# A quantised feed-forward stage: root mean square in the scale, more work on GpSimd, turned h one step later

## What is computed

```python
def rmsnorm(x, w):
    v = jnp.mean(jnp.square(x.astype(jnp.float32)), axis=-1, keepdims=True)
    x_hat = x * jax.lax.rsqrt(v + EPS_NORM)
    return (x_hat * w).astype(x.dtype)

def activation_quant(x):
    scale = 127.0 / jnp.clip(jnp.max(jnp.abs(x), axis=-1, keepdims=True), EPS_Q, None)
    return jnp.clip(jnp.round(x * scale), -128, 127) / scale
...
h = bitlinear(x, norm1_w, w1)
h = act_scale * jnp.square(jax.nn.relu(h)) + act_bias
y = bitlinear(h, norm2_w, w2)
```

## Time and profile before

| | us |
|---|---|
| median of 3 runs | 2208.47 |
| lowest, highest | 2199.37, 2210.56 |
| the profiled execution, its own time | 2208.38 |
| its span in the profile | 2206.4 |
| busy in the span: PE, DVE, ACT, POOL | 1934.4, 1438.6, 988.2, 937.7 |
| the last stage, first sum of squares to the end | 2018.5 to 2206.4 |

### The profile page before, as it was taken

How to read it: one execution, slowest core, us unless ns; L and a number is a source line. 1 busy time by engine, 2 the same in 40 slices (tenths; PEclk the granted TensorE clock), 3 DMA queues, 4 the chain that set the end, 5 groups by cost and what they waited for, 6 DMA issues and landing times. The chain is left out here.

```text
span 2206.4 us, 60606 instructions
## 1 busy us (share of the span) xinstructions
PE 1934.4 (88%) x21423; PEld 1458.4 (66%) x21426; DVE 1438.6 (65%) x3456; ACT 988.2 (45%) x1977; POOL 937.7 (42%) x978
## 2 busy tenths in 40 slices
PE   6999997997999489929999779999999999984675
PEld 3666666886888467728888657666767667652333
DVE  3666664775777634426676546776767777754998
ACT  2444442443111033413453335555555555534997
POOL 0111111221577723345655135656565565632333
PEclk8999997998999689968999879999999999985555
DMA  6211004995222199733331101101010101000111
GB/s 199 82 33 33 28 29 162 329 329 202 61 52 53 32 279 299 234 96 98 102 98 62 41 29 35 33 29 37 25 37 26 35 26 35 21 9 28 57 57 43
DMA packets 157099, 192.84 MB, mean 87 GB/s; under 512 B 27971, under 2 KB 140614, under 8 KB 157013
## 3 DMA queue, kind: packets, MB, share of 16 engines
q1 hardware_dynamic: 146741, 189.09, 27.3%
q0 software_dynamic: 10272, 2.62, 0.6%
HBM read 140.81 MB, written 77.51 MB: 99 GB/s over the span
## 5 line engine op out<-in xcount | busy, mean ns | idle before, releaser
L2960 DVE TENSOR_REDUCE xa_kq<-xa_A 100x4 f32<-100x1444 f32 x128 | 212.6, 1661 | 158.4 <-PE xa_A L2629 158.4
L2788 ACT ACTIVATE xa_prob<-xa_A 121x1600 f32<-121x1600 f32 x96 | 144.5, 1505 | 234.5 <-PE xa_A L2656 234.5
L2863 POOL TENSOR_TENSOR xa_prob<-xa_prob,xa_exp_bias 121x1600 f32<-121x1600 f32 x64 | 228.9, 3576 | 41.0 <-ACT xa_prob L2788 41.0
L1425 POOL DMA_INDIRECT slot_rows<-rt_x_again,rt_slot_u x150 | 155.2, 1035 | 67.7 <-issue 63.1
L2656 PEld LDWEIGHTS xa_A<-xa_q2T,xa_kqT 17*121 17x121 f32 x3072 | 92.3, 184 | 46.8 <-issue 29.7
L2888 POOL TENSOR_TENSOR xa_o_rstd<-xa_o_var,xa_power 100x1 f32<-100x1 f32 x32 | 17.8, 557 | 240.6 <-DVE xa_o_var L3000 240.6
L2629 PE MATMUL xa_A<-xa_kqT 16*100 16x361 f32 x1024 | 113.0, 511 | 6.8 <-ACT xa_prob L2788 6.8
L1671 POOL DMA_INDIRECT contrib<-ex_y,ex_place_u x64 | 62.4, 975 | 119.9 <-ACT ex_y L1723 107.1
L2656 PE MATMUL xa_A<-xa_q2T,xa_kqT 17*121 17x100 f32 x3072 | 108.5, 278 | 4.8 <-DVE xa_kq L2960 4.2
L717 DVE TENSOR_TENSOR sa_masked<-sa_A,sa_later_keys 100x1600 f32<-100x1600 f32 x32 | 58.4, 1824 | 73.1 <-PE sa_A L471 73.1
L2573 PE MATMUL xa_C<-xa_wk,xa_rows_T 128*121 128x256 f32 x384 | 103.7, 408 | 1.7 <-ACT xa_rows_T L2768 1.7
(11 more groups left out here) (353 smaller groups left out, 5115.9 us busy)
## 6 DMA issues: line engine op xcount, KB each, us to landing
ex_w<-in_w13T SPq DMA_DIRECT2D x64, 352.0 KB, 8.6
contrib<-xs_zero SPq DMA_DIRECT2D x30, 640.0 KB, 6.6
la_rows<-contrib SPq DMA_DIRECT2D x16, 1200.0 KB
xs_ctxT<-in_ctxT SPq DMA_DIRECT2D x32, 512.0 KB
xa_rows_t<-in_ctx SPq DMA_DIRECT2D x96, 121.0 KB
ex_w<-in_w2T SPq DMA_DIRECT2D x64, 176.0 KB
slot_rows<-xs_zero SPq DMA_DIRECT2D x32, 272.0 KB, 4.3
ex_x_t<-slot_rows SPq DMA_DIRECT2D x64, 136.0 KB, 6.1
```

What stands on the lines that cost most here:

```text
L1425: nc.gpsimd.indirect_dma_start(slot_rows, bass.IndirectOffsetOnAxis(slot_u[:, k, n:n + 1], 0), x_again[:, k, :], None, bounds_check=SLOTS ...
L2788: nc.scalar.activation(prob[:, n, :].rearrange("p (h a) -> p h a", h=HPG), A[:ROWS, :, 0:G * T], ACT.Exp, scale=EXP_SCALE).then_inc(exp_re ...
L2863: nc.gpsimd.tensor_tensor(chunk, chunk, exp_bias[:, n, :].unsqueeze(1).to_broadcast([ROWS, HEADS, T]), ALU.mult).then_inc(biased, 1)
L2960: nc.vector.tensor_reduce(kq[:T, k, NCH, 4 * j:4 * j + 4, DH:DH + 1].rearrange("p h o -> p (h o)"), A[:T, :, 0:src_len], axis=AXIS_X, op=A ...
```

## The change

The root mean square no longer multiplies x and h on VectorE. Rounding x/max(x) is the same with or without a common positive factor, so VectorE now scales the weighed but not normalised values, and the root enters the factors: `roots` raises the mean square to -0.5 and to 0.5 in one instruction of four numbers, `weigher` holds the first times the mean of the weights and the second times epsilon/127, and `scales` and `weigh` use them. `weigh_x` (x times weight) is on GpSimd, `weigh_h` stays on VectorE without the root. `whole_x` and `whole_h` go to GpSimd, `copy_x` goes from ScalarE to VectorE. `xn` and `hn` have two buffers each. TensorE and `copy_h` treat the h of the step before; `root_out` is one step later and first in GpSimd's list; `residual` comes behind `scale_h`. Line numbers after the change differ: `finish` is L3404, `weigh_h` L3376, `whole_h` L3202.

```diff
         ss = s.sb("ss", [P, 2, 2])
-        ms = s.sb("ms", [P, 2])
-        rms = s.sb("rms", [P, 2, 2])
-        power = s.sb("power", [P, 2])
+        ms = s.sb("ms", [P, 2, 2])
+        root = s.sb("root", [P, 2, 2])
+        factor = s.sb("factor", [P, 2, 2])
+        weigher = s.sb("weigher", [P, 2, 2, 2])
...
                 def rows(b):
                     k = b[1] % 2
                     sp.wait_ge(xn_ready, at(b, 1, -1))
+                    sp.wait_ge(x_squared, at(b, 1, -1))
                     sp.dma_start(x_t[:, k, :], x_tiles[b[0] * 2 + b[1]]).then_inc(x_loaded[k], 16)
...
             @block.gpsimd
             def _(pool):
-                for sem in (o_var_ready, o_rstd_ready):
+                for sem in (o_var_ready, o_rstd_ready, xn_ready, xi_ready, hi_ready):
                     pool.sem_inc(sem, LEAD)
                 pool.sem_inc(backw_ready, LEAD - 3)
-                nc.gpsimd.memset(power[:], -0.5)
+                nc.gpsimd.memset(power[:, 0, :], -0.5)
+                nc.gpsimd.memset(power[:, 1, :], 0.5)
+                nc.gpsimd.memset(factor[:, 0, :], 1.0)
+                nc.gpsimd.memset(factor[:, 1, :], EPS_Q / 127.0)
                 nc.gpsimd.memset(eps[:, 0:2], EPS_N)
                 nc.gpsimd.memset(eps[:, 2:3], LN_EPS).then_inc(power_set, 1)
                 pool.wait_ge(power_set, 1)
+                nc.gpsimd.tensor_tensor(factor[:, 0, :], factor[:, 0, :], wmean[:], ALU.mult).then_inc(power_set, 1)
+                pool.wait_ge(power_set, 2)
+
+                def weigh_x(b):
+                    k = b[1] % 2
+                    pool.wait_ge(x_loaded[k], loads_of(b, 1))
+                    nc.gpsimd.tensor_tensor(xn[:, k, :], x_t[:, k, :], n1[:], ALU.mult).then_inc(xn_ready, 1)
 
                 def weigh(b, has):
                     k = b[1] % 2
                         pool.wait_ge(relu_done, at(later(b, 1), 1, 1))
                     if has(-2):
                         pool.wait_ge(r_ready, at(later(b, -2), 1, 1))
-                    nc.gpsimd.tensor_tensor(backw[:, k, two], back[:, two], wmean[:, two], ALU.mult).then_inc(backw_ready, 1)
+                    pool.wait_ge(rms_ready, at(later(b, -1), 1, 1))
+                    if has(3):
+                        pool.wait_ge(x_turned, at(later(b, 2), 1, 1))
+                        pool.wait_ge(x_scaled, at(later(b, 3), 1, 1))
+                    nc.gpsimd.tensor_tensor(backw[:, k, two], back[:, two], weigher[:, 1 - k, 0, two], ALU.mult).then_inc(backw_ready, 1)
+
+                def whole_x(b):
+                    k = b[1] % 2
+                    nc.gpsimd.tensor_scalar(xi[:], xn[:, k, :], ROUND, 127.0, ALU.subtract, ALU.min).then_inc(xi_ready, 1)
+
+                def whole_h(b):
+                    k = b[1] % 2
+                    pool.wait_ge(h_turned, at(b, 1, 0))
+                    pool.wait_ge(h_scaled, at(b, 1, 1))
+                    nc.gpsimd.tensor_tensor(carry[:], eps[:, 0:1], eps[:, 0:1], ALU.add)
+                    nc.gpsimd.tensor_scalar(hi[:], hn[:, k, :], ROUND, 127.0, ALU.subtract, ALU.min).then_inc(hi_ready, 1)
 
                 def roots(b, has):
                     k = b[1] % 2
                     if has(1):
                         pool.wait_ge(h_summed, at(later(b, 1), 1, 1))
                     if b[1] > FIRST:
+                        pool.wait_ge(root_ready, at(later(b, -1), 1, 1))
+                    for copy in range(2):
+                        last = nc.gpsimd.tensor_tensor(ms[:, copy, two], ss[:, k, two], eps[:, two], ALU.add)
+                    last.then_inc(ms_ready, 1)
+                    pool.wait_ge(ms_ready, at(b, 1, 1))
+                    if b[1] > FIRST:
                         pool.wait_ge(rms_ready, at(later(b, -1), 1, 1))
-                    nc.gpsimd.tensor_tensor(ms[:, two], ss[:, k, two], eps[:, two], ALU.add).then_inc(ms_ready, 1)
-                    pool.wait_ge(ms_ready, at(b, 1, 1))
-                    if has(-1):
-                        pool.wait_ge(hn_ready, at(later(b, -1), 1, 1))
-                    if has(2):
-                        pool.wait_ge(xn_ready, at(later(b, 2), 1, 1))
-                    nc.gpsimd.tensor_tensor(rms[:, k, two], ms[:, two], power[:, two], ALU.pow).then_inc(rms_ready, 1)
+                    nc.gpsimd.tensor_tensor(root[:, :, two], ms[:, :, two], power[:, :, two], ALU.pow).then_inc(root_ready, 1)
+                    pool.wait_ge(root_ready, at(b, 1, 1))
+                    if has(-1) or has(2):
+                        pool.wait_ge(back_ready, at(later(b, -1), 1, 1))
+                    nc.gpsimd.tensor_tensor(weigher[:, k, :, two], root[:, :, two], factor[:, :, two], ALU.mult).then_inc(rms_ready, 1)
 
...
                 def body(b, has):
+                    if has(-2):
+                        root_out(later(b, -2))
+                    if has(4):
+                        weigh_x(later(b, 4))
                     if has(0) or has(3):
                         weigh(b, has)
+                    if has(3):
+                        whole_x(later(b, 3))
+                    if has(0):
+                        whole_h(b)
                     if has(1) or has(4):
                         roots(b, has)
-                    if has(-1):
-                        root_out(later(b, -1))
 
                 periods(pool, NT, FIRST, LAST, REACH, body)
 
                     last.then_inc(y_done, 1)
 
                 def body(b, has):
-                    if has(0):
-                        turn_h(b)
+                    if has(-1):
+                        turn_h(later(b, -1))
+                    if has(2):
+                        hidden(later(b, 2))
+                    if has(-1):
+                        down(later(b, -1))
                     if has(3):
                         turn_x(later(b, 3))
-                    if has(0):
-                        down(b)
-                    if has(3):
-                        hidden(later(b, 3))
 
                 periods(pe, NT, FIRST, LAST, REACH, body)
 
             @block.scalar
             def _(act):
-                for sem in (x_squared, relu_done, h_squared, h_summed, h_ready, xiT_ready, hiT_ready):
+                for sem in (x_squared, relu_done, h_squared, h_summed, h_ready, hiT_ready):
...
 
-                def copy_x(b):
-                    act.wait_ge(x_turned, at(b, 1, 1))
-                    act.wait_ge(h_done, at(b, 1, 0))
-                    nc.scalar.activation(xiT[:].rearrange("p c t -> p (c t)"), TX[:, 0:KC * P], ACT.Copy).then_inc(xiT_ready, 1)
-
                 def relu(b, slot):
...
                         relu(later(b, 1), k)
                     if has(1) or has(4):
                         if b[1] >= FIRST + 2:
-                            act.wait_ge(rms_ready, at(later(b, -2), 1, 1))
+                            act.wait_ge(ms_ready, at(later(b, -2), 1, 1))
                     if has(4):
                         square_x(later(b, 4), k)
+                    if has(-1):
+                        copy_h(later(b, -1))
                     if has(1):
                         square_h(later(b, 1))
                         sum_h(later(b, 1), k)
                         scale_h(later(b, 1))
-                    if has(0):
-                        copy_h(b)
-                    if has(3):
-                        copy_x(later(b, 3))
 
                 periods(act, NT, FIRST, LAST, REACH, body)
 
             @block.vector
...
-                def norm_h(b, slot):
+                def copy_x(b):
+                    dve.wait_ge(x_turned, at(b, 1, 1))
+                    dve.wait_ge(h_done, at(b, 1, 0))
+                    nc.vector.tensor_copy(xiT[:].rearrange("p c t -> p (c t)"), TX[:, 0:KC * P]).then_inc(xiT_ready, 1)
+
+                def weigh_h(b):
                     k = b[1] % 2
                     dve.wait_ge(h_ready, at(b, 1, 1))
-                    dve.wait_ge(rms_ready, at(later(b, -1), 1, 1))
-                    dve.wait_ge(hi_ready, at(b, 1, 0))
-                    nc.vector.scalar_tensor_tensor(hn[:], h[:, k, :], rms[:, slot, 0:1], n2[:], ALU.mult, ALU.mult).then_inc(hn_ready, 1)
-
-                def norm_x(b, slot):
-                    k = b[1] % 2
-                    dve.wait_ge(x_loaded[k], loads_of(b, 1))
-                    dve.wait_ge(rms_ready, at(later(b, -4), 1, 1))
-                    dve.wait_ge(xi_ready, at(b, 1, 0))
-                    nc.vector.scalar_tensor_tensor(xn[:], x_t[:, k, :], rms[:, slot, 1:2], n1[:], ALU.mult, ALU.mult).then_inc(xn_ready, 1)
+                    dve.wait_ge(hi_ready, at(later(b, -2), 1, 1))
+                    nc.vector.tensor_tensor(hn[:, k, :], h[:, k, :], n2[:], ALU.mult).then_inc(hn_ready, 1)
 
...
-
-                def scales(b, has):
+                    nc.vector.tensor_reduce(amax[:, 1:2], xn[:, k, :], axis=AXIS_X, op=ALU.max, apply_absolute_value=True).then_inc(x_max, 1)
+
+                def scales(b, has, slot):
                     two = pair(has, 0, 3)
```

(31 more changed lines are left out.)

24 lines of the change are left out of this document (14 added, 10 removed).

## The result

The change makes the kernel slower by 3.8%: 2290.1 us (2286.57 to 2294.01 in 4 runs) against 2209.5 of the kernel before on the same chip (2199.37 to 2212.87 in 4 runs), ratio 1.038 with an interval of 1.035 to 1.041. The forecast was 2218.4 with 2193 to 2243 as its range, so the time lies far above it, and also above the 2250 of rival 2.

A forecast was written before the change was run, and what follows sets the result against it. VectorE was taken to bound the kernel, ScalarE next; a new ring through GpSimd sums to 7.22 us a step against 6.77, so 0.45 x 22 = 10 us lost: 2208.4 + 10 = 2218.4 us, range 2193 to 2243.

The forecast's parts named there:

- rival 2: GpSimd's `tensor_scalar` costs what its two-input work costs: `whole_h` 2.31 us, 8.69 us a step, 2250 us; chance 0.20.
- What bounds the kernel before: Last stage: VectorE runs through, busy 47.21 of 50 us, ScalarE next at 45.57; steps 6.77 us apart.
- the ring of the new order: Last stage, once per step: `finish`, scales, GpSimd's passes, `ms`, root, `o_rstd`, `finish`; 7.22 us against 6.77.
- `whole_h` 1.05: GpSimd's pass taking the offset out of h, 1024 wide, in the ring: 1.05 us.
- `whole_x` 0.40: GpSimd's pass taking the offset out of x, 256 wide, in the ring: 0.40 us.
- the 7.22: Sum in us of the ring's seven links, one step of the last stage, against 6.77 before.
- `weigh_h` holds up `ms`, 1.10: VectorE's `weigh_h` takes the ports when `whole_h` ends, so GpSimd's `bf_ms` waits 1.10 us in the ring.
- exclude each other for their whole length: Port rule for VectorE and GpSimd instructions: the blocked one pays only its streaming part afterwards.
- ScalarE, TensorE and SP at nothing: Last stage: ScalarE's 5.79 us fits the longer step, TensorE's new order is hidden, SP's extra wait long satisfied.
- C: Theory in the follow-up runs: new order, copy of x or root of four numbers causes the loss; h_dve over 2265 us.
- Rival 1: The ports don't bind in the ring; ScalarE's 6.1 us sets the step, 15 us gained, 2193 us; chance 0.24.
- Rival 3: Shifting turned h only lengthens the tail, or next x waits for `copy_x`: 0 to +8 us; chance 0.04.

The follow-up runs named there:

- x_dve: Changed kernel with only the offset of x taken out by VectorE again, h's pass still on GpSimd: 2264.0 us, ratio to before 1.021 to 1.028.
- h_cast: Changed kernel with GpSimd's pass over h as a plain copy to bf16, offset and upper bound left out: 2240.3 us, ratio to before 1.009 to 1.016.
- h_sub: Changed kernel with GpSimd's pass over h as a subtract of a constant tile, upper bound left out: 2276.4 us, ratio to before 1.025 to 1.032.
- h_dve: Changed kernel with only the offset of h taken out by VectorE again: 2211.5 us, ratio to before 0.9994 to 1.0031.
- turn_back: hx_dve with the turning of h, its product and ScalarE's copy back in the step that scales h: 2211.7 us, ratio to before 0.9983 to 1.0018.
- hx_dve: Changed kernel with the offsets of both h and x taken out by VectorE again: 2202.9 us, ratio to before 0.9956 to 0.9980.
- f16_new: Changed kernel with scaled values written as fp16 plus 1536, offset taken off in the PSUM copies, no bound of 127: 2187.6 us, ratio to before 0.9855 to 0.9913.
- ints8: Changed kernel with VectorE scaling x and h into 8-bit integers and GpSimd only copying them to bf16: 2246.3 us, ratio to before 1.013 to 1.018.
- price: Kernel before plus extra GpSimd instructions on idle buffers, alone and beside VectorE, to tell durations: one run, 2248.2 us.
- b_h: Kernel before with one edit, the offset of h taken out by GpSimd behind the weighing of the scales: 2295.0 us, ratio to before 1.034 to 1.041.

## Why the prediction was wrong, point by point

- **What bounds the kernel before, and the ring of the new order**: right. Every link of the ring is in the trace in the place foretold; `finish` is held by `weigh_x` (0.70 to 0.81 us for 0.40), `backw` arrives behind `scale_h` and ends 0.05 us behind it, `o_rstd` to `o_rstd` closes once a step.
- **The step that failed** is the term `whole_h` 1.05 (and `whole_x` 0.40) with its bounds. It was put between "from below: the memsets" and "from above: the two-input instructions", 0.95 to 2.31 us, by the thought that an instruction with one tensor can't cost more than one with two. It took 3.62 (and 1.07): +2.57 and +0.67 of the 2.69 us by which the turn of 9.91 missed the 7.22, with 0.55 us in gaps, in `backw` and in the root, less the 1.10 of the collision that didn't come. The same two passes are what the forecast missed by pricing the first and last steps at nothing: behind the last `bf_hi` the span is 2.9 us longer, and the pass itself is 2.9 longer (3.62 for 0.69); ahead of the first it is 2.7, which is gone in x_dve (its stage begins 16.5 us ahead of the first `bf_hi`, the changed kernel's 20.1, that of before 16.7). The ends of a range that come from other operations don't bound this one, since here the operation sets the rate: two constants 3.63, one 2.78, none 1.04, for the same tile. The Trainium skill ("GPSIMD Engine Reference", section "Engine selection") calls one-input work roughly line-rate. The copy (1.04 us for 1024 elements) goes well with that; the arithmetic with constants is at 2.7 to 3.5 times its time. The measurement decides, and the estimate of 0.85 us from that page would have missed by more.
- **`weigh_h` holds up `ms`, 1.10**: right as a mechanism and in size (0.98 in h_cast and h_sub), absent in the changed kernel itself, where the pass outlasts the multiply.
- **"A VectorE `tensor_scalar` ... or one with two SBUF inputs, and a GpSimd instruction exclude each other for their whole length"**: too wide. It holds for GpSimd's two-tensor subtract, where VectorE ended 1.07 and 0.55 us behind 2.34, and there the Trainium skill ("SBUF — State Buffer", section "Who interferes with whom"), by which the first gets the pair for the whole instruction, agrees. Neither this nor that rule holds for its pass with constants, where the measurement decides: VectorE's instructions ended 1.5 to 2.5 us before GpSimd's.
- **ScalarE, TensorE and SP at nothing**: right for the loss (C fell with h_dve). The turning of h one step later isn't nothing where both passes are on VectorE: turn_back shows it there as a gain of 4 to 7 us. That the ring hides it in the changed kernel is argued, not shown.
- **The rivals**: rival 2 named the mechanism (GpSimd's `tensor_scalar` is dear) and stopped at the two-input rate, so its 8.69 us a step and 2250 fell short of 10.1 and 2290. It had 0.20; "against: those all read two tensors" was the wrong reason to keep it low. Rival 1 had one part right: `whole_h` does let VectorE's multiply through, after 1.0 us, and so the 1.10 is not in the ring. Its gain didn't follow, as the pass alone cost 2.57 more, and `finish` (0.83 for 0.78), h_cast's and h_sub's rows show that the ports do bind elsewhere. Rival 3 did not occur: in hx_dve, with the new order and both passes on VectorE, the first `bf_hi` comes 16.1 us into the stage and the last 10.1 before its end, for 16.7 and 10.1 in the kernel before.
- **The range** was built from the same two bounds, so it could not hold the time.

## What to carry to other kernels

An instruction that has no row of its own on that engine has no upper bound from its neighbours; before a large tile is moved to GpSimd, one kernel with the very form, alone and beside VectorE, prices it (here 3.63 us against VectorE's 0.69). An offload pays only if the other engine's queue has nothing behind it that the first engine waits for: VectorE was rid of 1.5 us of work a step (and got 0.3 of copying) and the step grew by 3.3, because the root that it waits for stood behind the pass. And look whether a pass can go altogether: letting the format of the write round, and the copy that exists anyway take the offset off, was faster in f16_new than every placement of the pass that was tried.

## What the runs showed of the hardware that was not expected

- GpSimd, 128 partitions by 1024 elements from fp32, alone: subtract and minimum with two constants 3.63 to 3.65 us, subtract with one 2.78, subtract of two tiles 2.34, copy to bf16 1.04; a copy from 8-bit integers took 1.03 in ints8. By the two widths of the first, (3.63 - 1.07) / 768 = 3.3 ns an element. Output in fp32 or bf16 made no difference. Once it had started, VectorE beside it lengthened it little or not at all (3.63 in price and the changed kernel, 3.63 to 3.70 in b_h); the 256-wide one took 1.52 in h_dve, where VectorE's `bf_hi` was in its way.
- While that pass runs, VectorE's instructions that share ports with GpSimd are held only until about 1.0 us after its start (price, x_dve). That this is close to the 1.04 us of the bare copy may mean that its reading is over by then; no run here tests it.
- VectorE's write to fp16 of a value near 1536, and to 8-bit integers, rounds to whole numbers at no extra time (0.748 us for 128x1024 in each, as for fp32), and TensorE turns fp16 tiles as it does bf16.
